# Graph network layers on one core: one-hots of 128-edge tiles built and summed over 64 columns instead of 128

## The chip, the cores and the metric

The kernel runs on one core of a Trainium2 chip. The metric is the time of one execution on the device, in microseconds (us). Five engines work side by side: PE (TensorE, with PEld for its weight loads), DVE (VectorE), ACT (ScalarE), POOL (GpSimd) and SP (SyncE), each with its own instruction stream; semaphores hold them together.

## The reference, cut to what matters

A graph of 6250 nodes with 128 features and 100,000 edges that are sorted by destination goes through two graph-convolution layers, a normalisation, an attention layer over the same edges, and a second normalisation. Each layer sums, for each node, the rows of its edges:

```python
deg = segment_sum(ew, dst)                       # degree, then dinv = rsqrt(deg + 1)
norm = dinv[src] * ew * dinv[dst]                # layers 1 and 2 (with self-loops)
out = segment_sum((x @ W)[src] * norm[:, None], dst) + b
...
e = zs @ aw[0] + zd @ aw[1] + rh @ aw[2]         # attention layer; zs = z[src], rh = r_h @ fc_r_w.T
alpha = softmax of leaky_relu(e) over the edges of a node
agg = segment_sum(alpha[:, None] * (zs + rh), dst)
```

## The kernel before

**Tiles and windows.** The edges are cut into 782 tiles of 128 (T), in 98 groups of 8 (GT, G). Since the edges are sorted, the destinations of one tile lie close together. Each tile t has a window of W = 128 nodes that begins at `base(t)`, 8t - 60, cut at both ends of the graph. `rankC[:, t]` holds for each of the tile's edges its destination less the window's start. A one-hot of a tile is a matrix of 128 edges by 128 window columns, with the edge's weight where the column is its rank. The sum over a tile is one matmul: the 128 gathered rows (or edge features) are the stationary operand, the one-hot is the moving one, and the result is added to 128 columns of a PSUM bank, from `column(t)`.

**Stages.** The *degree pass* builds bf16 one-hots (`SH`, 16 buffers of a group), three groups of four on DVE (L1571) and one on ACT (L1191 and L1195), and sums edge weights with them on PE (L811), in pieces where a window straddles a 512-column bank. ACT copies each closed bank out, and `dinv` and the scaled rows x1 follow. The *first and second pass* (p = 0, 1) are the convolution layers: DVE builds f32 one-hots with weights (`build_S`, L1608, 4 buffers of a group), PE sums with them (`sum_group`, L858). The *third pass* (p = 2) is the attention layer: each tile has two sums, over the gathered rows (L858) and over the edge features (L860), with attention weights that DVE, PE and ACT make per chunk of four groups in front of them.

**Gathers.** The source rows are fetched by POOL with one indirect DMA a tile (L720) into a ring of 18 groups (12 in the third pass); POOL waits until PE has summed the group whose place it needs. The first 18 groups of the first pass are fetched from x itself, ahead of x1; the table of each later pass must be stored first.

**Far sets.** To have fewer gathers, some groups (24 in the first pass, 36 in the second, 12 in the third) are not gathered: their rows are looked up by matmuls with one-hots of source nodes (L898, in the third pass L1033, L1020, L1029) and summed with 288-column one-hots (L1681 on DVE, L910 on PE; in the third pass L1375 and L1380 on ACT, L1045 on PE). These one-hots and sums are not part of the change.

**The general path.** `find_odd` tests on the device whether every rank fits its window (and two other conditions). If not, a flag is set, and a second, general path computes everything anew.

**Order.** The order is written out by hand: each engine's stream loops over groups, with the far sets' steps put between them at fixed groups. The lines to follow are these:

```python
def base(t):
    return min(max(GT * t - MARGIN, 0), NP - W)
...
for j, t in enumerate(tiles(SEQ[gg][1])):                      # build_S, DVE
    last = v.tensor_scalar(S[:, gg % NS, j, :], iota[:, :], rankC[:, t:t + 1], w[:, t:t + 1], ALU.is_equal, ALU.mult)
last.then_inc(s("S_built"), 1)
```

Of the kernel before, what the change touches and what calls it, by code (L numbers as in the profile page):

```python
# [7 lines left out]
ALU = mybir.AluOpType  # L8
ACT = mybir.ActivationFunctionType
AX = mybir.AxisListType  # L10

N, E, D = 6250, 100000, 128
P = 128
W = 128
GT = 8
T = -(-E // P)
G = -(-T // GT)
TC = G * GT
# [7 lines left out]
BW = 512  # L26
NK = -(-NP // BW)
MARGIN = (W - GT) // 2
R = 18
R0 = 18  # L30
NS = 4
NR = 8
ND = 16
# [14 lines left out]
def base(t):  # L48
    return min(max(GT * t - MARGIN, 0), NP - W)

# [2 lines left out]
    return range(q * GT, min((q + 1) * GT, T))  # L53


def pieces(t):

    b, out = base(t), []
    for k in range(b // BW, (b + W - 1) // BW + 1):
        lo, hi = max(b, k * BW), min(b + W, (k + 1) * BW)  # L60
        out.append((k, lo - k * BW, hi - k * BW, lo - b))
    return out

# [12 lines left out]
NA = -(-NP // BA)  # L76
# [16 lines left out]
def column(t):  # L93

    return base(t) - bank_of(t) * BA


OPENS = [min(t for t in range(T) if bank_of(t) == k) for k in range(NA)]
# [139 lines left out]
def build(nc, x, src, dst, edge_attr, edge_weight, W1, b1, W2, b2, fc_w, fc_r_w, attn_w, loop_w, out):  # L238
    ctx = ExitStack()
    with ctx:  # L240
# [19 lines left out]
        iota = sb("iota", [P, P])  # L260
# [4 lines left out]
        iota_h = sb("iota_h", [P, P], BF16)  # L265
        pidx = sb("pidx", [P, 1])
        ident = sb("ident", [P, P])
        ones = sb("ones", [P, P])
# [9 lines left out]

        ring = sb("ring", [P, R, GT, XW])
        rows = sb("rows", [P, NB, XW])  # L280
        SR = sb("SR", [P, NS + NR, GT, W])
        S, rh = SR[:, 0:NS], SR[:, NS:NS + NR]
        SH = SR[:, 0:ND // 2].rearrange("p s t w -> p (s t w)").bitcast(BF16).rearrange("p (s t w) -> p s t w", s=ND, t=GT)
# [13 lines left out]
        rankC = sb("rankC", [P, TC])  # L297
# [71 lines left out]

        setup = ring[:, R - 7:R].rearrange("p s t d -> p (s t d)")  # L370
        lanes = [setup[:, k * EB * P:(k + 1) * EB * P].rearrange("p (b t) -> p b t", t=P) for k in range(5)]
# [4 lines left out]
        tmpC = setup[:, 5 * EB * P + 2 * TC:5 * EB * P + 3 * TC]  # L376
# [38 lines left out]
        ps = [ctx.enter_context(nc.psum_tensor(f"ps{k}", [P, BW], FP32)) for k in range(8)]  # L415
# [3 lines left out]
        def s(name):  # L419
            if name not in sems:  # L420
                sems[name] = sem(name)
            return sems[name]
# [15 lines left out]
        def ring_at(p, h):  # L438

            return (AT[p] + h) % R if p < 2 else GATHERED.index(h) % R2  # L440

# [253 lines left out]
        def _(pool):  # L695
# [5 lines left out]
            nc.gpsimd.memset(rows[:, NB - 1, 0:D], 0.0).then_inc(s("pads_set"), 1)  # L701
            nc.gpsimd.iota(baseI, [[GT, TC]], base=-MARGIN, channel_multiplier=0).then_inc(s("iota_made"), 1)

# [51 lines left out]
        def _(pe):  # L755
# [44 lines left out]
            for q in range(G):  # L800
# [4 lines left out]
                for j, t in enumerate(tiles(q)):  # L805
                    for k, lo, hi, w0 in pieces(t):
                        if t == FIRST[k]:
                            if k >= 2:
                                pe.wait_ge(s("deg_evac"), k - 1)
                            clear(ps[6 + k % 2][0:3, :], 3)  # L810
                        last = nc.tensor.matmul(ps[6 + k % 2][0:3, lo:hi], ewP[:, t, :], SH[:, q % ND, j, w0:w0 + hi - lo],  # L811
                                                start=False, stop=t == LAST[k])
# [29 lines left out]
            def sum_group(p, h):  # L842
                gg = AT[p] + h
                q = SEQ[gg][1]
                parts = PARTS[q] if p < 2 and q in PARTS else (0, len(tiles(q)))
                if p == 2:
                    pe.wait_ge(rh_loaded[q % NR], rh_turns(q))
                pe.wait_ge(s("S_built"), gg + 1)
                near = p < 2 or q in GATHERED
                for j, t in enumerate(tiles(q)):  # L850
                    if near and j in parts:
                        await_rows(pe, p, tiles(q)[j:parts[parts.index(j) + 1]])
                    k = bank_of(t)
                    if t == OPENS[k] and (p == 2 or k + 1 < NA):
                        open_bank(p, k)
                    at, stop = slice(column(t), column(t) + W), t + 1 in OPENS or t + 1 == T and p < 2
                    if near:
                        last = nc.tensor.matmul(ps[(p * NA + k) % 2][:, at], ring[:, ring_at(p, h), j, 0:D], S[:, gg % NS, j, :], start=False, stop=stop)  # L858
                    if p == 2:
                        last = nc.tensor.matmul(ps[2 + k % 2][:, at], rh[:, q % NR, j, :], S[:, gg % NS, j, :], start=False, stop=stop)  # L860
                last.then_inc(s("summed"), 1)

            def count_before(s_, g):
# [312 lines left out]
        def _(act):  # L1176
# [7 lines left out]
            for i, q in enumerate(DEG_ACT):  # L1184
                for k in range(NK):
                    if q - 4 < CLOSE[k] + 3 <= q:
                        evacuate_deg(k)
                if q >= ND:
                    act.wait_ge(s("deg_summed"), q - ND + 1)
                for j, t in enumerate(tiles(q)):  # L1190
                    last = nc.scalar.activation(SH[:, q % ND, j, :], iota_h[:, :], ACT.Abs, bias=rankC[:, t:t + 1], scale=-1.0)  # L1191
                last.then_inc(s("deg_onehot_act"), 1)
                act.wait_ge(s("deg_onehot_act"), 2 * i + 1)
                n = len(tiles(q))
                nc.scalar.activation(SH[:, q % ND, 0:n, :], SH[:, q % ND, 0:n, :], ACT.Relu, bias=ones[:, 0:1], scale=-1.0).then_inc(s("deg_onehot_act"), 1)  # L1195
            for k in range(NK):
                if CLOSE[k] + 3 > DEG_ACT[-1]:
                    evacuate_deg(k)
# [5 lines left out]
            for c in range(0, NB, 7):  # L1204
                for b in range(c + 4, c + 7):
                    last = nc.scalar.activation(rows[:, b, 0:D], rows[:, b, 0:D], ACT.Copy, scale=dinv[:, b:b + 1])
# [257 lines left out]
        def _(dve):  # L1464
            v = nc.vector
            steps = [0]

            def link(ins):

                steps[0] += 1  # L1470
                ins.then_inc(s("dve_step"), 1)
                dve.wait_ge(s("dve_step"), steps[0])
# [20 lines left out]
            at, got = cols_from(0, 1)  # L1493
# [5 lines left out]
            for first, n in ((0, 4), (4, EB - 4)):  # L1499
                at, got = cols_from(first, n)  # L1500
                v.tensor_tensor(rankC[:, at], got, baseT[:, at], ALU.subtract).then_inc(s("cols_copied"), 1)
            for first, n in ((0, 4), (4, EB - 4)):
                at, got = cols_from(first, n)
# [7 lines left out]
            for first, n in ((1, 4), (5, EB - 5)):  # L1511
                at, got = cols_from(first, n)
# [31 lines left out]
            def find_odd():  # L1544

                link(v.tensor_tensor(tmpC, rankC[:, :], baseT, ALU.add))
                link(v.tensor_tensor(dstF.rearrange("p b t -> p (b t)")[:, 0:T - 1], tmpC[:, 0:T - 1], tmpC[:, 1:T], ALU.is_equal))
                link(v.tensor_reduce(odd[:, 0:1], dstF.rearrange("p b t -> p (b t)")[:, 0:T - 1], AX.X, ALU.max))
                link(v.tensor_scalar(tmpC, rankC[:, :], 0.0, None, ALU.is_lt))
                link(v.tensor_reduce(odd[:, 1:2], tmpC[:, 0:T], AX.X, ALU.max))  # L1550
                link(v.tensor_scalar(tmpC, rankC[:, :], float(W), None, ALU.is_ge))
                link(v.scalar_tensor_tensor(tmpC, rankC[:, :], FAR / 2, tmpC, ALU.is_lt, ALU.mult))
                link(v.tensor_reduce(odd[:, 2:3], tmpC[:, 0:T], AX.X, ALU.max))
                link(v.tensor_scalar(dlowI, srcR, P - 1, None, ALU.bitwise_and))
                link(v.tensor_copy(slowH, dlowI))
                link(v.tensor_scalar(dlowI, dstR, P - 1, None, ALU.bitwise_and))
                v.tensor_copy(dlowH, dlowI).then_inc(s("dlo_made"), 1)
                v.tensor_reduce(odd[:, 3:4], odd[:, 0:3], AX.X, ALU.max).then_inc(s("odd_found"), 1)
                dve.wait_ge(s("odd_found"), 1)
                dve.sem_inc(s("setup_done"), 1)  # L1560
# [6 lines left out]
            for q in DEG_DVE:  # L1567
                if q >= ND:
                    dve.wait_ge(s("deg_summed"), q - ND + 1)
                for j, t in enumerate(tiles(q)):  # L1570
                    last = v.tensor_scalar(SH[:, q % ND, j, :], iota_h[:, :], rankC[:, t:t + 1], None, ALU.is_equal)  # L1571
                last.then_inc(s("deg_onehot"), 1)
                if q == 0:
                    weights()
                if q == 2 * ND:
                    find_odd()
# [11 lines left out]
            for i, t0 in enumerate(SAT):  # L1588
                last = v.tensor_scalar(firstC[:, i:i + 1], firstC[:, i:i + 1], float(base(t0)), 0.0, ALU.subtract, ALU.max)
# [3 lines left out]
            for c in range(0, NB, 7):  # L1593
                for b in range(c, c + 4):
                    last = v.tensor_scalar(rows[:, b, 0:D], rows[:, b, 0:D], dinv[:, b:b + 1], None, ALU.mult)
# [7 lines left out]
            def build_S(p, h, w):  # L1603
                gg = AT[p] + h
                if gg >= NS:
                    dve.wait_ge(s("summed"), gg - NS + 1)
                for j, t in enumerate(tiles(SEQ[gg][1])):
                    last = v.tensor_scalar(S[:, gg % NS, j, :], iota[:, :], rankC[:, t:t + 1], w[:, t:t + 1], ALU.is_equal, ALU.mult)  # L1608
                last.then_inc(s("S_built"), 1)

            def make_hi(s_, g):
# [273 lines left out]
            for r, i in enumerate(XR):  # L1885
                last = v.tensor_scalar(dstN[:, r, :], slotD[:, i, :], -1.0, None, ALU.mult)
# [228 lines left out]
            with any_wide(dve):  # L2115
# [16 lines left out]
                for b in range(NB):  # L2132
                    last = v.tensor_scalar(rows[:, b, 0:D], rows[:, b, 0:D], dinv[:, b:b + 1], None, ALU.mult)
# [11 lines left out]
                z = S[:, 1]  # L2145
# [114 lines left out]
```

## Time and profile before

| | |
|---|---|
| median of 3 runs | 2409.7 us (2406.36 to 2409.96) |
| span of the profiled execution, from its first to its last instruction | 3348.6 us |
| mean granted TensorE clock in it | 0.787 |
| PE / DVE / ACT / POOL busy | 2044.2 / 1834.8 / 946.7 / 1718.9 us |
| degree pass, first, second, third pass (begin, us) | about 45, 310, 1180, 2280 |

The profile is of one execution that was recorded instruction by instruction; its span is much longer than the time of a run, and the page gives no other time for it, so its span is its own time here. Busy times are of the profiled execution. The granted clock is the share of 2.4 GHz that TensorE was given: 0.50 is 1.2 GHz, 1.00 is 2.4 GHz.

### The profile page before, as it was taken

To read this page: it belongs to the slowest core of one execution; us is meant where nothing else is said; L and a number is where in the kernel's file an instruction comes from. 1 tells how busy PE (TensorE), PEld (TensorE's weight loads), DVE (VectorE), ACT (ScalarE), POOL (GpSimd) and SP (SyncE) were. 2 spreads that over 40 slices of the span, in tenths; PEclk is the share of its full clock that TensorE was granted. 3 is DMA by queue.
4 is the path that set the end of the run, shared out by engine and by line. 5 is a ranking of instruction groups with operands and counts; after the bars stand their busy time and mean duration, and the time that the engine had idled before them with its cause. 6 is when DMAs were issued, how large, how long until landed. Compare 5 with 4: busy or idle time off the path is not lost.

```text
span 3348.6 us, 40819 instructions
## 1 busy us (share of the span) xinstructions
PE 2044.2 (61%) x13384; PEld 1762.3 (53%) x13384; DVE 1834.8 (55%) x7005; ACT 946.7 (28%) x1754; POOL 1718.9 (51%) x1781
## 2 busy tenths in 40 slices
PE   1416444588888911177777888106677667756786
PEld 1315433566767811166666677005666666645675
DVE  3626435577779810156656687217654564546457
ACT  1316000122233300033333444101254225412541
POOL 7351666665550067466556500555766646663640
PEclk9857667798999955588988899557778778877888
DMA  4112221222221122123333332525343534443431
GB/s 118 30 42 66 69 61 47 61 61 63 60 62 32 51 76 53 41 74 86 99 103 102 93 91 80 138 62 147 97 103 97 134 93 102 108 117 79 103 97 34
DMA packets 272093, 270.54 MB, mean 81 GB/s; under 512 B 43454, under 2 KB 218709, under 8 KB 271862
## 3 DMA queue, kind: packets, MB, share of 16 engines
q1 hardware_dynamic: 201790, 143.87, 15.1%
q0 software_dynamic: 56640, 117.52, 14.8%
q10 hardware_dynamic: 13448, 6.47, 0.7%
q8 instruction: 112, 1.84, 0.2%
q14 instruction: 103, 0.84, 0.1%
HBM read 254.14 MB, written 13.97 MB: 80 GB/s over the span
## 4 chain that ended last, share of the span: by engine, by line
PE 35%; DVE 21%; another core or an unknown queue 21%; issue 15%; ACT 4%; SPq 1%; DMA 1%; POOL 1%; ACTq 0%; DVEq 0%; POOLq 0%
PE ps L858 9%; PE ps L910 8%; DVE SR L1608 5%; PE ps L860 3%; PE ps L898 3%; PE ps L1045 2%; DVE U L1709 2%; DVE SR L1681 2%; DVE SR L1571 1%; PE ps L885 1%; DVE U L1648 1%; PE ps L1029 1%; POOL ring L720 1%; PE ps L792 1%
## 5 line engine op out<-in xcount | busy, mean ns | idle before, releaser
L720 POOL DMA_INDIRECT ring<-x_d,srcC x1132 | 1109.7, 980 | 971.2 <-issue 579.0
L858 PE MATMUL ps<-SR,ring 128*128 128x128 f32 x3540 | 672.5, 320 | 205.0 <-issue 132.0
L858 PEld LDWEIGHTS ps<-SR,ring 128*128 128x128 f32 x3540 | 580.5, 231 | 238.9 <-issue 178.9
L720 POOL DMA_INDIRECT ring<-h_d,srcC x494 | 469.9, 951 | 457.1 <-DMA h_d<-Lb 170.9
L1681 DVE TENSOR_SCALAR SR<-iota_r,cols 128x288 f32<-128x288 f32 x735 | 365.0, 564 | 303.9 <-remote 226.6
L910 PE MATMUL ps<-SR 128*128 128x288 f32 x1470 | 416.6, 435 | 118.1 <-ACT SR L1232 75.3
L910 PEld LDWEIGHTS ps<-SR 128*128 128x128 f32 x1470 | 292.3, 205 | 212.7 <-ACT SR L1232 77.5
L860 PE MATMUL ps<-SR 128*128 128x128 f32 x1564 | 340.3, 312 | 40.8 <-issue 34.6
L1232 ACT COPY SR<-ps 128x512 f32<-128x512 f32 (+1 forms) x195 | 106.0, 561 | 758.4 <-remote 502.9
L860 PEld LDWEIGHTS ps<-SR 128*128 128x128 f32 x1564 | 279.6, 228 | 48.3 <-issue 48.0
L898 PE MATMUL ps<-rows,SR 128*128 128x128 f32 x1470 | 196.2, 285 | 122.5 <-ACT SR L1241 90.6
L898 PEld LDWEIGHTS ps<-rows,SR 128*128 128x128 f32 x1470 | 186.7, 200 | 134.0 <-ACT SR L1241 96.0
L1608 DVE TENSOR_SCALAR SR<-iota,rankC,ewC 128x128 f32<-128x128 f32 x940 | 253.3, 357 | 2.6 <-DVE U L1812 1.1
L1608 DVE TENSOR_SCALAR SR<-iota,rankC,cols 128x128 f32<-128x128 f32 x782 | 213.0, 355 | 14.7 <-issue 11.7
L720 POOL DMA_INDIRECT ring<-in_x_dram,srcC x144 | 137.3, 953 | 93.7 <-issue 90.5
L1571 DVE TENSOR_SCALAR SR<-iota_h,rankC 128x128 bf16<-128x128 bf16 x584 | 107.6, 260 | 125.9 <-issue 106.1
L1709 DVE SCALAR_TENSOR_TENSOR U<-SR,v2B 128x128 f32<-128x128 f32 x686 | 156.0, 286 | 34.3 <-DVE U L1709 18.1
L1239 ACT ACTIVATE SR<-SR,negp 128x512 bf16<-128x512 bf16 (+1 forms) x195 | 134.9, 692 | 112.0 <-remote 100.3
L811 PE MATMUL ps<-SR,cols 128*3 128x128 bf16 (+2 forms) x974 | 74.0, 237 | 110.7 <-issue 57.0
L1241 ACT ACTIVATE SR<-SR,negp 128x512 f32<-128x512 bf16 (+1 forms) x195 | 135.9, 697 | 6.4
L1963 DVE TENSOR_TENSOR_SCAN U<-U,ps 32x384 f32<-32x384 f32 (+2 forms) x27 | 25.4, 942 | 203.8 <-remote 115.7
L811 PEld LDWEIGHTS ps<-SR,cols 128*3 128x3 bf16 x974 | 60.0, 96 | 123.5 <-issue 65.0
(288 smaller groups left out, 2703.4 us busy)
## 6 DMA issues: line engine op xcount, KB each, us to landing
SR<-in_edge_attr_dram SPq DMA_DIRECT2D x97, 512.0 KB
SR<-low_d SPq DMA_DIRECT2D x90, 256.0 KB
U<-dlo_d SPq DMA_DIRECT2D x74, 256.0 KB
ring<-x_d,srcC POOLq DMA_INDIRECT x1132
ring<-h_d,srcC POOLq DMA_INDIRECT x494
SR<-dlo_d SPq DMA_DIRECT2D x12, 512.0 KB
ring<-in_edge_attr_dram SPq DMA_DIRECT2D x12, 512.0 KB
U<-lo_d SPq DMA_DIRECT2D x18, 256.0 KB
```

Of the source, the lines that this page charges most:

```text
L720: pool.indirect_dma_start(ring[:, ring_at(p, h if p < 2 else q), k, 0:width], None, (x if p == 0 and h < R0 else table)[:, :], bass.Indire ...
L811: last = nc.tensor.matmul(ps[6 + k % 2][0:3, lo:hi], ewP[:, t, :], SH[:, q % ND, j, w0:w0 + hi - lo], start=False, stop=t == LAST[k])
L858: last = nc.tensor.matmul(ps[(p * NA + k) % 2][:, at], ring[:, ring_at(p, h), j, 0:D], S[:, gg % NS, j, :], start=False, stop=stop)
L860: last = nc.tensor.matmul(ps[2 + k % 2][:, at], rh[:, q % NR, j, :], S[:, gg % NS, j, :], start=False, stop=stop)
L898: last = nc.tensor.matmul(ps[3 + m % 2][:, i * P:(i + 1) * P], ohS[:, m % 2, i * P:(i + 1) * P], rows[:, a, 0:D], start=True, stop=True)
L910: nc.tensor.matmul(ps[5][:, SLACK:SPAN], rowX[:, m % 2, i * P:(i + 1) * P], slotS[:, n % NQ, :], start=False, stop=a == NB - 1).then_inc(s ...
L1239: nc.scalar.activation(low, low, ACT.Abs, bias=negp[:, 0:1]).then_inc(s("low_apart"), 1)
L1241: return nc.scalar.activation(out, low, ACT.Relu, bias=negp[:, 1:2], scale=-1.0)
L1571: last = v.tensor_scalar(SH[:, q % ND, j, :], iota_h[:, :], rankC[:, t:t + 1], None, ALU.is_equal)
L1608: last = v.tensor_scalar(S[:, gg % NS, j, :], iota[:, :], rankC[:, t:t + 1], w[:, t:t + 1], ALU.is_equal, ALU.mult)
L1681: v.tensor_scalar(slotS[:, n % NQ, :], iota_up, slotD[:, RUNS[i], a:a + 1], slotW[:, RUNS[i], a:a + 1], ALU.is_equal, ALU.mult).then_inc(s ...
L1709: v.scalar_tensor_tensor(junk[:, n % NJ, :], attr, 1.0, v2B[:, :], ALU.mult, ALU.mult, accum_out=s2C[:, t:t + 1]).then_inc(s("rh_dotted"), 1)
```

## The change

Inner tiles (all but the first and last eight) get a narrower view of their window, its columns 32 to 95. One-hots are built over these 64 columns alone and summed into these 64 alone; edge tiles keep 128. This holds in the degree pass (DVE, ACT and PE, whose pieces are cut from the view) and in the three passes (`build_S` and `sum_group`). The windows' starts, the banks and their order, the number of one-hots and of sums in the three passes and the far sets stay. `find_odd` compares the ranks of inner tiles with 32 and 96 in place of 0 and 128, with three instructions for each of the two tests in place of one, so that the general path is taken where the narrow view would miss an edge.

```diff
+NEAR, EDGE = W // 4, GT
...
+def view(t):
+
+    return (NEAR, W - NEAR) if EDGE <= t < T - EDGE else (0, W)
...
     b, out = base(t), []
-    for k in range(b // BW, (b + W - 1) // BW + 1):
-        lo, hi = max(b, k * BW), min(b + W, (k + 1) * BW)
+    a, z = (b + w for w in view(t))
+    for k in range(a // BW, (z - 1) // BW + 1):
+        lo, hi = max(a, k * BW), min(z, (k + 1) * BW)
...
-                    at, stop = slice(column(t), column(t) + W), t + 1 in OPENS or t + 1 == T and p < 2
+                    lo, hi = view(t)
+                    at, stop = slice(column(t) + lo, column(t) + hi), t + 1 in OPENS or t + 1 == T and p < 2
                     if near:
-                        last = nc.tensor.matmul(ps[(p * NA + k) % 2][:, at], ring[:, ring_at(p, h), j, 0:D], S[:, gg % NS, j, :], start=False, stop=stop)
+                        last = nc.tensor.matmul(ps[(p * NA + k) % 2][:, at], ring[:, ring_at(p, h), j, 0:D], S[:, gg % NS, j, lo:hi], start=False, stop=stop)
                     if p == 2:
-                        last = nc.tensor.matmul(ps[2 + k % 2][:, at], rh[:, q % NR, j, :], S[:, gg % NS, j, :], start=False, stop=stop)
+                        last = nc.tensor.matmul(ps[2 + k % 2][:, at], rh[:, q % NR, j, :], S[:, gg % NS, j, lo:hi], start=False, stop=stop)
...
-                    last = nc.scalar.activation(SH[:, q % ND, j, :], iota_h[:, :], ACT.Abs, bias=rankC[:, t:t + 1], scale=-1.0)
+                    lo, hi = view(t)
+                    last = nc.scalar.activation(SH[:, q % ND, j, lo:hi], iota_h[:, lo:hi], ACT.Abs, bias=rankC[:, t:t + 1], scale=-1.0)
...
-                nc.scalar.activation(SH[:, q % ND, 0:n, :], SH[:, q % ND, 0:n, :], ACT.Relu, bias=ones[:, 0:1], scale=-1.0).then_inc(s("deg_onehot_act"), 1)
+                nc.scalar.activation(SH[:, q % ND, 0:n, lo:hi], SH[:, q % ND, 0:n, lo:hi], ACT.Relu, bias=ones[:, 0:1], scale=-1.0).then_inc(s("deg_onehot_act"), 1)
...
-                link(v.tensor_scalar(tmpC, rankC[:, :], 0.0, None, ALU.is_lt))
+                for a, z in ((0, EDGE), (EDGE, T - EDGE), (T - EDGE, TC)):
+                    last = v.tensor_scalar(tmpC[:, a:z], rankC[:, a:z], float(view(a)[0]), None, ALU.is_lt)
+                link(last)
...
-                    last = v.tensor_scalar(SH[:, q % ND, j, :], iota_h[:, :], rankC[:, t:t + 1], None, ALU.is_equal)
+                    lo, hi = view(t)
+                    last = v.tensor_scalar(SH[:, q % ND, j, lo:hi], iota_h[:, lo:hi], rankC[:, t:t + 1], None, ALU.is_equal)
...
-                    last = v.tensor_scalar(S[:, gg % NS, j, :], iota[:, :], rankC[:, t:t + 1], w[:, t:t + 1], ALU.is_equal, ALU.mult)
+                    lo, hi = view(t)
+                    last = v.tensor_scalar(S[:, gg % NS, j, lo:hi], iota[:, lo:hi], rankC[:, t:t + 1], w[:, t:t + 1], ALU.is_equal, ALU.mult)
```

## Rows read from the trace of the kernel before

**Rows 1.** The page, part 1: busy us, share of span, instructions.

```profile
PE 2044.2 (61%) x13384; PEld 1762.3 (53%) x13384; DVE 1834.8 (55%) x7005; ACT 946.7 (28%) x1754; POOL 1718.9 (51%) x1781
```

**Rows 2.** The page, part 4: chain that ended last, by engine, by line.

```profile
PE 35%; DVE 21%; another core or an unknown queue 21%; issue 15%; ACT 4%; SPq 1%; DMA 1%; POOL 1%; ACTq 0%; DVEq 0%; POOLq 0%
PE ps L858 9%; PE ps L910 8%; DVE SR L1608 5%; PE ps L860 3%; PE ps L898 3%; PE ps L1045 2%; DVE U L1709 2%; DVE SR L1681 2%; DVE SR L1571 1%; PE ps L885 1%; DVE U L1648 1%; PE ps L1029 1%; POOL ring L720 1%; PE ps L792 1%
```

**Rows 3.** Timeline of DVE, then PE: start us, us, operation, count, idle before.

```profile
107.34 22.52 DVE L1571 TENSOR_SCALAR SR<-iota_h,rankC 128x128 bf16<-128x128 bf16 x138 [0.45 <-issue]
...
188.40 0.26 DVE L1571 TENSOR_SCALAR SR<-iota_h,rankC 128x128 bf16<-128x128 bf16 x1 [1.01 <-issue]
189.80 0.26 DVE L1571 TENSOR_SCALAR SR<-iota_h,rankC 128x128 bf16<-128x128 bf16 x1 [1.15 <-issue]
...
1215.76 0.37 PE L898 MATMUL ps<-rows,SR 128*128 128x128 f32 x1 [2.43 <-issue]
```

**Rows 4.** Timeline of POOL, the start of the second pass: one gather.

```profile
1194.79 0.94 POOL L720 DMA_INDIRECT ring<-h_d,srcC  x1 [0.30 <-issue]
```

**Rows 5.** Groups by line: busy us, mean ns, idle us before and releasers.

```profile
L720 POOL DMA_INDIRECT ring<-x_d,srcC x1132 | 1109.7, 980 | 971.2 <-issue 579.0 <-PE ps L860 175.2 <-remote 129.4
L858 PE MATMUL ps<-SR,ring 128*128 128x128 f32 x3540 | 672.5, 320 | 205.0 <-issue 132.0 <-DVE SR L1608 54.7 <-remote 11.0
L860 PE MATMUL ps<-SR 128*128 128x128 f32 x1564 | 340.3, 312 | 40.8 <-issue 34.6 <-DVE SR L1608 6.0
L1608 DVE TENSOR_SCALAR SR<-iota,rankC,ewC 128x128 f32<-128x128 f32 x940 | 253.3, 357 | 2.6 <-DVE U L1812 1.1 <-issue 0.3
...
L1571 DVE TENSOR_SCALAR SR<-iota_h,rankC 128x128 bf16<-128x128 bf16 x584 | 107.6, 260 | 125.9 <-issue 106.1 <-remote 19.4
```

**Rows 6.** Windows: us; PE, PEld, DVE, ACT, POOL busy (x); granted clock, DMA, GB/s.

```profile
700.00:1180.00 480.00, 401.62 (x2544) 344.92 (x2544) 365.82 (x1119) 149.37 (x270) 180.49 (x186) 0.93 0.20 55
1400.00:2095.00 695.00, 548.19 (x3481) 464.29 (x3482) 456.31 (x1503) 272.19 (x429) 311.30 (x326) 0.89 0.33 90
2310.00:3300.00 990.00, 685.66 (x4134) 610.27 (x4134) 560.46 (x2575) 368.60 (x703) 561.36 (x569) 0.79 0.40 103
```

**Rows 7.** Groups by line and shape, DVE: other widths.

```profile
L1681 DVE TENSOR_SCALAR SR<-iota_r,cols 128x288 f32<-128x288 f32 x735 | 365.0, 564 | 303.9 <-remote 226.6 <-PE ps L910 77.1
L1825 DVE TENSOR_SCALAR U<-U,pidx 128x1024 bf16<-128x1024 bf16 x74 | 33.1, 483 | 97.4 <-remote 87.2 <-PE ps L944 6.3 <-DMA U<-dlo_d 3.5
...
L1802 DVE SCALAR_TENSOR_TENSOR s1C<-U,ds,s1n 128x16 f32<-128x16 f32 x48 | 8.5, 231 | 0.9 <-DVE ds L1797 0.3
```

**Rows 8.** Timeline of PE in the degree pass: one group's sums.

```profile
141.28 1.01 PE L811 MATMUL ps<-SR,cols 128*3 128x128 bf16 x8 [6.57 <-DVE SR L1571]
```

**Rows 9.** Timeline of PE, third pass: a stretch of narrow and wide matmuls.

```profile
2727.16 3.65 PE L1029 MATMUL ps<-ring 128*128 128x49 f32 x16
2730.61 3.75 PE L860 MATMUL ps<-SR 128*128 128x128 f32 x16
2734.15 2.12 PE L1029 MATMUL ps<-ring 128*128 128x49 f32 x16
2736.10 2.02 PE L860 MATMUL ps<-SR 128*128 128x128 f32 x16
2738.25 1.09 PE L1029 MATMUL ps<-ring 128*128 128x49 f32 x8
2740.17 1.09 PE L1029 MATMUL ps<-ring 128*128 128x49 f32 x8 [0.83 <-ACT ring L1363]
2741.10 3.42 PE L860 MATMUL ps<-SR 128*128 128x128 f32 x16
```

**Rows 10.** Chain by line in 700:1180, 1400:2095 and 2310:3300 us, in this order.

```profile
by line: PE ps L910 17.9%; PE ps L858 13.7%; another core or an unknown queue 8.5%; PE ps L885 6.9%; PE ps L898 6.6%; DVE SR L1608 6.5%; issue 5.5%; DVE SR L1681 4.3%; DVE U L1648 4.2%; PE ps L872 3.6%; DVE U L1637 2.2%; PE ps L840 2.0%; PE
by line: PE ps L910 26.1%; PE ps L858 15.9%; issue 11.9%; another core or an unknown queue 10.3%; PE ps L898 9.5%; DVE SR L1608 4.5%; DVE SR L1681 3.5%; ACT SR L1239 2.1%; PE ps L944 1.4%; PE ps L840 1.3%; SPq L505 1.0%; ACT L1293 0.9%; ACT
by line: issue 17.8%; another core or an unknown queue 13.5%; PE ps L858 9.5%; PE ps L860 9.4%; PE ps L1045 6.6%; DVE U L1709 5.5%; DVE SR L1608 5.0%; PE ps L1029 2.7%; PE ps L1033 2.5%; PE ps L1020 2.2%; DVE U L1970 1.6%; DVE U L1972 1.6%;
```

More of the change, by code:

```diff
@@ L1548, in find_odd @@
                 link(v.tensor_reduce(odd[:, 0:1], dstF.rearrange("p b t -> p (b t)")[:, 0:T - 1], AX.X, ALU.max))
-                link(v.tensor_scalar(tmpC, rankC[:, :], 0.0, None, ALU.is_lt))
+                for a, z in ((0, EDGE), (EDGE, T - EDGE), (T - EDGE, TC)):
+                    last = v.tensor_scalar(tmpC[:, a:z], rankC[:, a:z], float(view(a)[0]), None, ALU.is_lt)
+                link(last)
                 link(v.tensor_reduce(odd[:, 1:2], tmpC[:, 0:T], AX.X, ALU.max))
-                link(v.tensor_scalar(tmpC, rankC[:, :], float(W), None, ALU.is_ge))
+                for a, z in ((0, EDGE), (EDGE, T - EDGE), (T - EDGE, TC)):
+                    last = v.tensor_scalar(tmpC[:, a:z], rankC[:, a:z], float(view(a)[1]), None, ALU.is_ge)
+                link(last)
                 link(v.scalar_tensor_tensor(tmpC, rankC[:, :], FAR / 2, tmpC, ALU.is_lt, ALU.mult))
```

## The prediction

> **What bounds the kernel now.** I read the page's busy line first, then its chain of waits, then the gathers one by one, then each stage with its clock. No engine is full: PE is busy 61% of the span, DVE 55%, POOL 51% [rows 1]. The span, 3348.6 us, is not the time of a run: the three runs have a median of 2409.7 us (2406.36 to 2409.96), 939 us less. The chain shows where such an excess can lie: 21% of it is "another core or an unknown queue" and 15% "issue" [rows 2], together 1229 us that belong to no engine's work. While POOL gathers without a break, DVE steps once in 1.40 us with "issue" before each step, and PE pauses 2.43 us before one matmul; where POOL is held up, DVE issues 138 one-hots in 22.52 us, 163 ns each [rows 3]. I read these pauses as the price of recording and not as work. So engine work on the chain carries over into a run in full, and "issue" and "unknown" do not: terms are worked out in the profiled span and added to 2409.7 us unscaled.
>
> A gather is issued every 1.25 us (0.94 us and a gap of 0.30) [rows 4], also when nothing holds it up. There are 1770 of them (1132 from x1 and x2 [rows 5], and two more rows of L720 with 494 and 144): 1770 x 1.25 = 2212 us. If that holds in a run, only 198 us of the 2409.7 us are left for all times in which POOL waits. The gathers are thus a floor that no engine's saving gets under, and a cover that can swallow small changes of PE or DVE. Above that floor PE and DVE take turns: in 700 to 1180 us (the second half of the first pass) PE is busy 402 of 480 us and DVE 366; in the third pass 686 and 560 of 990 [rows 6].
>
> **What the change removes, on DVE.** build_S (L1608) has 1866 instructions: 940 of them in one row [rows 5], 782 and 144 in two more. Sixteen edge tiles in each of three passes keep 128 columns, so 1818 shrink. A 128-column one costs 253.3 us / 940 = 269 ns of busy time. No row shows 64 columns of this kind. From the 16-column two-operation row (8.5 us / 48 = 177 ns) the slope is 0.82 ns a column, a saving of 53 ns; from the 288-column row (365.0 / 735 = 497 ns) it is 1.42 ns, a saving of 91 ns [rows 7]. I take 60, nearer the row with the same plain columns, since the 288-column one reads a reversed view. DVE's busy time falls by 1818 x 60 ns = 109 us (bounds 96 and 165). Only what is on the chain counts: L1608 is 5% of it [rows 2], 164 us, of which 60/269 go: **-37 us** (bounds: 0 if the gathers cover it, -109 if every build is in the way).
>
> In the degree pass L1571 takes 107.6 us / 584 = 184 ns for 128 bf16 columns [rows 5], and 33.1 us / 74 = 447 ns for 1024 [rows 7]: 0.29 ns a column, 19 ns for 64, 11 us in all. It is 1% of the chain, 44 us, of which 19/184 go: **-5 us** (bounds 0 and -11; zero if the 144 gathers ahead, 180 us, end after this stage does). PE's degree matmuls get narrower and fewer (974 pieces become 880, counted from the tiles' bounds, since fewer windows straddle a bank), and ACT's one-hots shrink too. Both are costed at nothing: PE is waiting for DVE's one-hots there (6.57 us before one group) [rows 8], and ACT has a quarter of the groups. If that cover were gone they would give some us more. find_odd gains four small instructions, under 0.3 us each by the 16-column row's 231 ns [rows 7]: **+1 us**.
>
> **What it does not remove, on PE.** The sums (L858 and L860, 3540 + 1564 instructions [rows 5]) keep their stationary operand, 128 columns of f32 rows; only the moving one-hot shrinks. The row to read is a stretch where sixteen matmuls with 49 moving columns alternate with sixteen of 128: 3.65 and 3.75 us at the one clock, 2.12 and 2.02 us at the other [rows 9]. A matmul with 49 columns takes as long as one with 128. So 64 columns take as long as 128, and PE's sums save **0 us**.
>
> A page gives another figure. The Trainium skill, "TensorE: Matmul & The Clock Gate", section "Back-to-back issue gap", has the gap of matmuls follow the moving columns, 134 cycles for 128 and about 60 for 64; by it the sums would lose about half of their PE time. The trace does not agree: 2.12 against 2.02 us.
>
> **What it may cost, on PE's clock.** The same rows show something worse. At 1.2 GHz sixteen 49-column matmuls ran back to back for 3.65 us, and the clock was still 1.2 GHz after them (the next sixteen took 3.75 us); after those sixteen of 128 columns it was 2.4 GHz. Then two batches of eight 49-column matmuls ran with a gap of 0.83 us, and the 128-column ones behind them took 3.42 us, the low clock again [rows 9]. Narrow matmuls keep PE as occupied as wide ones but do not hold the clock up. The granted clock is 0.93 in 700 to 1180 us, 0.89 in the second pass, 0.79 in the third [rows 6]. The first two also have sums of 288 columns (L910) and look-ups of 128 (L898), which stay; the third is mostly L858 and L860. I take 0.91, 0.86 and 0.69: in the third pass a third of the way down to 1.2 GHz (0.50), because its far sets (L1045, L1033) still bring wide matmuls in 39 of 98 groups (three rounds of 13 look-ups in the code). PE's lines on the chain [rows 10] are, in the order of stages, 51% of 480 us (L910, L858, L885, L898, L872, L840) = 243 us; 54% of 695 (L910, L858, L898, L944, L840) = 377; 33% of 990 (L858, L860, L1045, L1029, L1033, L1020) = 326. Cost: 243 x (0.93/0.91 - 1) = 5; 377 x (0.89/0.86 - 1) = 13; 326 x (0.79/0.69 - 1) = 47: **+65 us**. Bounds: 0 if the clock stays, 326 x (0.79/0.50 - 1) = 189 us in the third pass if it runs at 1.2 GHz throughout.
>
> The Trainium skill, same page, section "Part 1: The HAM clock gate", says the clock follows how busy the PE has recently been. By that rule sixteen narrow matmuls back to back would raise the clock as sixteen wide ones do, this term would be zero and the time that of the first rival, 2369 us. The rows speak against it, though no row here has 64 columns.
>
> **Sum:** -37 - 5 + 1 + 65 = +24 us: 3348.6 becomes 3373 in a profiled run, and 2409.7 becomes 2434 us in a timed one. I forecast 2434.
>
> **The rivals.**
> *The clock holds and DVE's saving shows* (faster). 64 columns are more than 49, and in a run without the recording pauses the matmuls stand closer, which holds the clock. Then the sum is -41: 2369 us. For it: PE waits on L1608 54.7 us at L858 [rows 5]. Against it: the rows of 49 columns. It decides if the third pass's clock stays above about 0.74: there 326 x (0.79/0.74 - 1) = 22 us and the 18 us of the other stages together eat DVE's 41. If all of DVE's 109 + 11 us counted, the time would be 2290 us, but POOL's 2212 us and its waits at the ends of three passes (an estimate: some 30 us each) leave little under 2300.
> *The gathers cover both.* If POOL is the floor in the second and third pass, a shorter DVE and a slower PE both vanish behind it, since the ring holds 18 groups (12 in the third pass). For it: 2212 of 2409.7 us. Against it: in the trace POOL waits for L860 175.2 us [rows 5]. Time: 2405 to 2414 us.
> *PE's sums get cheaper after all.* At 2.4 GHz sixteen sums take 2.02 us [rows 9], 126 ns each; if 64 columns halved that, 5000 instructions would give 315 us, and the gathers' floor would stop it at about 2300 us. Against it: the 49-column rows. (The Trainium skill's figure for the gap, above, would have it so.)
> *The general path is taken.* Not with these inputs: worked out from the reference's setup, the ranks in inner tiles lie between 55 and 86, inside 32 to 95. Under 1 in 100, and then many times the time.
>
> **How the numbers follow.** Forecast (the clock falls by more than DVE saves): 0.48, its own range 2415 to 2520. Clock holds: 0.34, 2300 to 2404. Covered: 0.15. Cheaper sums: 0.03. Faster is 0.34 + 0.03 = 0.37, same 0.15, slower 0.48; a change within 0.2% (4.8 us) can't be told from none. For 8 in 10 I leave out about a tenth on each side: below 2340 us (most of DVE's saving and cheaper sums) and above 2505 us (about half of the bound of 189 us for the third pass).
>
> **What would show it.** L1608 at about 210 ns busy each instead of 269, L1571 at 165; sixteen L858 in about 2.0 us at the high clock and 3.6 at the low one as now; the granted clock of the third pass near 0.69, of the first two within 0.03 of now; more POOL waits for L858 and L860. The prediction is wrong if the clock of the third pass stays at 0.79, if sixteen sums take visibly less than 2 us at the high clock, or if POOL's gathers fill the run so that nothing moves.

## The result, and the profile after

The changed kernel takes a median of 2475.78 us in five runs (2470.48 to 2479.55), the kernel before 2408.41 us beside it (2405.29 to 2409.96). The ratio is 1.0274 with a 95% interval of 1.0258 to 1.029: 66 us slower. The forecast was 24 us slower, so the sign and the range hold and the size does not.

The profile of the changed kernel has a span of 2474.0 us, which is the time of its run. First the page: its busy line, its line of granted clocks in 40 slices, its chain by engine, and groups by line.

```profile
PE 2049.2 (83%) x13290; PEld 1823.9 (74%) x13290; DVE 1751.1 (71%) x7009; ACT 928.4 (38%) x1754; POOL 1745.8 (71%) x1781
...
PEclk9975789799999689889999965556866589556876
...
PE 46%; DVE 21%; POOL 16%; issue 9%; ACT 3%; DMA 3%; SPq 1%; ACTq 0%; DVEq 0%; POOLq 0%
...
L866 PE MATMUL ps<-SR,ring 128*128 128x64 f32 (+1 forms) x3540 | 671.9, 327 | 65.9 <-DVE SR L1623 35.3
...
L868 PE MATMUL ps<-SR 128*128 128x64 f32 (+1 forms) x1564 | 379.8, 346 | 5.7 <-DVE SR L1623 5.7
...
L1623 DVE TENSOR_SCALAR SR<-iota,rankC,ewC 128x64 f32<-128x64 f32 (+1 forms) x940 | 224.4, 336 | 2.2 <-DVE U L1827 0.6
```

The rows of before that stand ahead of the prediction cannot be set beside these, because that execution was stretched to 3348.6 us [rows 1 to 3]. I took that for the price of recording. It was not: a second profile of the same kernel has a span of 2402.3 us, and every comparison below is with it. The same lines of its page:

```profile
PE 1834.3 (76%) x13384; PEld 1623.4 (68%) x13384; DVE 1815.0 (76%) x7005; ACT 946.3 (39%) x1754; POOL 1749.5 (73%) x1781
...
PEclk9878899999999899999999995778897889779988
...
POOL 40%; PE 21%; issue 17%; DVE 12%; DMA 8%; ACT 1%; SPq 1%; ACTq 0%; POOLq 0%; DVEq 0%
...
L858 PE MATMUL ps<-SR,ring 128*128 128x128 f32 x3540 | 613.8, 305 | 105.0 <-DVE SR L1608 55.5
...
L860 PE MATMUL ps<-SR 128*128 128x128 f32 x1564 | 320.1, 300 | 6.0 <-DVE SR L1608 6.0
L1608 DVE TENSOR_SCALAR SR<-iota,rankC,ewC 128x128 f32<-128x128 f32 x940 | 254.9, 360 | 2.2 <-DVE U L1812 0.5
```

Three things are to be seen. In an undisturbed execution the chain of before is POOL's: 40%, and most of the 17% "issue" is the 0.30 us between two gathers. After the change PE holds 46% of it. The narrow sums are busy for longer than the wide ones (671.9 + 379.8 against 613.8 + 320.1 us), and the clock line falls to 5 and 6 in the third pass. DVE's one-hots fall from 254.9 / 940 = 271 ns to 239.

Now the passes by windows, from the first sum to the last (columns as in [rows 6]). Before, measured again:

```profile
155.00:809.00 654.00, 545.37 (x3905) 482.07 (x3904) 553.66 (x1711) 172.81 (x312) 477.86 (x475) 0.91 0.28 79
828.00:1448.00 620.00, 528.35 (x3595) 459.39 (x3594) 462.85 (x1517) 276.42 (x434) 466.76 (x484) 0.93 0.43 120
1503.00:2391.00 888.00, 645.62 (x4467) 589.29 (x4468) 604.08 (x2820) 381.18 (x727) 650.95 (x658) 0.85 0.48 126
```

After:

```profile
147.00:808.00 661.00, 581.79 (x3906) 516.26 (x3905) 534.88 (x1711) 172.77 (x312) 478.07 (x480) 0.85 0.30 79
827.00:1446.00 619.00, 546.22 (x3595) 471.52 (x3594) 448.60 (x1512) 276.21 (x435) 464.08 (x484) 0.90 0.43 119
1506.00:2462.00 956.00, 810.75 (x4468) 747.10 (x4468) 580.13 (x2814) 383.85 (x727) 654.98 (x658) 0.67 0.46 116
...
1515.00:1680.00 165.00, 134.97 (x614) 128.69 (x615) 94.64 (x437) 41.15 (x85) 126.90 (x126) 0.50 0.44 111
...
1877.00:1977.00 100.00, 88.89 (x394) 82.53 (x394) 65.64 (x302) 34.26 (x74) 77.14 (x76) 0.50 0.45 109
```

The loss is the third pass: 956 against 888 us, at a clock of 0.67 against 0.85. It has stretches of 100 us and more that run wholly at 1.2 GHz (0.50), with PE busy 82 to 89% of the time.

POOL's timeline shows where such a slower PE becomes time. Columns are start, length, operation, and the idle time before it. Before, measured again, the last gather of a pass and the first of the next:

```profile
776.40 0.98 POOL L720 DMA_INDIRECT ring<-x_d,srcC  x1 [0.30 <-issue]
814.92 0.95 POOL L720 DMA_INDIRECT ring<-h_d,srcC  x1 [37.54 <-issue]
...
1441.44 0.95 POOL L720 DMA_INDIRECT ring<-h_d,srcC  x1 [0.30 <-DMA ring<-h_d,srcC]
1465.03 1.10 POOL L720 DMA_INDIRECT ring<-x_d,srcC  x1 [22.63 <-issue]
...
2354.22 0.96 POOL L720 DMA_INDIRECT ring<-x_d,srcC  x1 [0.30 <-issue]
```

After:

```profile
769.27 1.83 POOL L727 DMA_INDIRECT ring<-x_d,srcC  x1 [0.30 <-issue]
813.95 0.94 POOL L727 DMA_INDIRECT ring<-h_d,srcC  x1 [42.86 <-issue]
...
1437.35 0.94 POOL L727 DMA_INDIRECT ring<-h_d,srcC  x1 [0.30 <-issue]
1466.74 1.10 POOL L727 DMA_INDIRECT ring<-x_d,srcC  x1 [28.45 <-issue]
...
2366.66 0.94 POOL L727 DMA_INDIRECT ring<-x_d,srcC  x1 [0.30 <-issue]
```

Inside a pass the gathers run at one per 1.25 us in both kernels. At the end of a pass POOL has nothing to do until PE has worked off the groups that lie in the ring and the pass's rows are stored. I call this time the drain. For the third pass it is the time from the start of the last gather (2354.22 and 2366.66) to the end of PE's last sums (2391.7 and 2462.9), which are these, before and after:

```profile
2391.36 0.39 PE L860 MATMUL ps<-SR 128*128 128x128 f32 x2
...
2462.22 0.64 PE L868 MATMUL ps<-SR 128*128 128x128 f32 x2
```

How far PE is behind can be counted: from the last gather on, it has some 165 of the third pass's sums still to start before the change, and some 370 after. The drains of all kernels profiled (of one execution each), in us, and each kernel's ratio to before (of its timed runs):

| kernel | first | second | third | sum | ratio (95%) |
|---|---|---|---|---|---|
| before, again | 38.5 | 23.6 | 37.5 | 99.6 | 1 |
| the change | 44.7 | 29.4 | 96.2 | 170.3 | 1.0274 (1.0258 to 1.029) |
| builds 64, sums 128 | 33.7 | 22.6 | 34.3 | 90.6 | 0.993 (0.9908 to 0.9952) |
| the same, second time | 28.0 | 22.9 | 35.7 | 86.6 | 0.9936 (0.9923 to 0.995) |
| builds 128, sums 64 | 78.9 | 32.1 | 93.6 | 204.6 | 1.0386 (1.0341 to 1.0432) |
| third pass 128 | 62.6 | 28.4 | 45.3 | 136.3 | 1.0059 (1.0035 to 1.0082) |
| degree pass alone 64 | 41.0 | 22.4 | 42.3 | 105.7 | 1.0001 (0.9988 to 1.0013) |
| 96 in place of 64 | 46.1 | 30.7 | 42.3 | 119.1 | 0.9997 (0.9981 to 1.0014) |
| change + one-row matmuls | 63.8 | 27.6 | 150.4 | 241.8 | 1.1292 (1.1246 to 1.1338) |
| change + 128-row matmuls | 63.8 | 28.4 | 71.6 | 163.8 | 1.0206 (1.0186 to 1.0226) |
| builds 40, sums 128 | 33.7 | 21.6 | 35.3 | 90.6 | 0.9926 (0.9908 to 0.9943) |
| builds 64 in first pass alone | 32.6 | 23.4 | 38.5 | 94.5 | 0.9955 (0.9943 to 0.9967) |
| builds 64 in third pass alone | 41.5 | 24.6 | 33.1 | 99.2 | 1.0001 (0.9993 to 1.001) |

The change adds 170.3 - 99.6 = 71 us of drain, and the two profiled spans differ by 2474.0 - 2402.3 = 72 us. The stretches between the drains nearly cancel: the gathers of the first pass end 7 us earlier, those of the second take 3 us less and those of the third 11 us more. Drains of one kernel differ by some 5 us between profiles (33.7 and 28.0 above), so smaller differences in the table are not read.

### The profile page after: what moved, and what is told of

Its sections match the earlier page's. It is cut to its first block, busy times and chain, and to the rows that moved or that the text cites. A ratio compares the mean times of both kernels' runs of the same rounds, so it can differ in the third digit from the quotient of the medians.

```text
span 2474.0 us, 40635 instructions
## 1 busy us (share of the span) xinstructions
PE 2049.2 (83%) x13290; PEld 1823.9 (74%) x13290; DVE 1751.1 (71%) x7009; ACT 928.4 (38%) x1754; POOL 1745.8 (71%) x1781
## 4 chain that ended last, share of the span: by engine, by line
PE 46%; DVE 21%; POOL 16%; issue 9%; ACT 3%; DMA 3%; SPq 1%; ACTq 0%; DVEq 0%; POOLq 0%
POOL ring L727 16%; PE ps L866 13%; PE ps L918 9%; PE ps L868 6%; DVE SR L1623 4%; DVE SR L1585 4%; PE ps L906 3%; PE ps L893 2%; DVE SR L1696 2%; PE ps L1053 2%; PE ps L1037 2%; DVE U L1663 1%; PE ps L799 1%; DMA ring<-x_d,srcC 1%; PE ps L847 1%
## 5 line engine op out<-in xcount | busy, mean ns | idle before, releaser
L727 POOL DMA_INDIRECT ring<-x_d,srcC x1132 | 1126.3, 995 | 381.2 <-issue 364.3
L866 PE MATMUL ps<-SR,ring 128*128 128x64 f32 (+1 forms) x3540 | 671.9, 327 | 65.9 <-DVE SR L1623 35.3
L866 PEld LDWEIGHTS ps<-SR,ring 128*128 128x128 f32 x3540 | 607.2, 243 | 89.5 <-issue 48.2
L868 PE MATMUL ps<-SR 128*128 128x64 f32 (+1 forms) x1564 | 379.8, 346 | 5.7 <-DVE SR L1623 5.7
L918 PEld LDWEIGHTS ps<-SR 128*128 128x128 f32 x1470 | 294.3, 206 | 82.8 <-issue 3.6
L868 PEld LDWEIGHTS ps<-SR 128*128 128x128 f32 x1564 | 320.7, 260 | 6.0 <-issue 5.8
L1623 DVE TENSOR_SCALAR SR<-iota,rankC,ewC 128x64 f32<-128x64 f32 (+1 forms) x940 | 224.4, 336 | 2.2 <-DVE U L1827 0.6
L1623 DVE TENSOR_SCALAR SR<-iota,rankC,cols 128x64 f32<-128x64 f32 (+1 forms) x782 | 185.7, 331 | 7.1 <-PE ps L868 5.8
L1053 PE MATMUL ps<-ring 128*128 128x288 f32 x294 | 104.8, 512 | 0.0
L799 PE MATMUL ps<-iota_r,zero_h 1*128 1x512 bf16 (+1 forms) x128 | 58.8, 484 | 51.2 <-DVE SR L1623 34.1
L1663 DVE TENSOR_SCALAR U<-iota,U 128x128 f32<-128x128 f32 x288 | 61.0, 298 | 54.7 <-PE ps L893 54.7
```

The costliest lines, as they stand in the source:

```text
L727: pool.indirect_dma_start(ring[:, ring_at(p, h if p < 2 else q), k, 0:width], None, (x if p == 0 and h < R0 else table)[:, :], bass.Indire ...
L918: nc.tensor.matmul(ps[5][:, SLACK:SPAN], rowX[:, m % 2, i * P:(i + 1) * P], slotS[:, n % NQ, :], start=False, stop=a == NB - 1).then_inc(s ...
L1053: nc.tensor.matmul(ps[5][:, SLACK:SPAN], rowX2[:, m % 2, j * P:(j + 1) * P], slotX[:, n % NQ2, :], start=False, stop=a == NB - 1).then_inc ...
L1623: last = v.tensor_scalar(S[:, gg % NS, j, lo:hi], iota[:, lo:hi], rankC[:, t:t + 1], w[:, t:t + 1], ALU.is_equal, ALU.mult)
```

## The experiments

**The kernel before once more.** No edit.

> The kernel before once more, unchanged, for a profile of its own. My reading in the prediction (the long span of 3348.6 us is the price of recording): the pauses come again and the span is again some 3300 us. Rival (that one execution was stretched by something else): the span comes out at about 2406 us, like the 2474.0 us of the changed kernel beside its 2475.8 us, and the stages can then be set side by side.

Its span is 2402.3 us, its time 2404.21. The rival holds: the pauses of [rows 3] belonged to that one execution. The shares of its chain [rows 2, 10], which sized three of my terms, describe no ordinary run.

**Builds narrow, sums wide.**

```
 sum_group:
-                    lo, hi = view(t)
+                    lo, hi = 0, W
 build_S:
+                wide = gg < NS or any(view(t) == (0, W) for t in tiles(SEQ[gg - NS][1]))
-                    lo, hi = view(t)
+                    lo, hi = (0, W) if wide else view(t)
```

> One-hots are still built in 64 columns by DVE (in 128 in the first four groups and after an edge group, so that the outer columns hold zeros), but PE sums over all 128. Theory 1 (narrow sums lower the clock, and that is the loss): the clock of the third pass comes back to what the kernel before has, DVE keeps its saving of about 30 ns an instruction (269 to 239 ns), and the time is at or under the one before: 2375 to 2410 us. Theory 2 (the narrow builds or their strided one-hots cost, whatever PE does): it stays at 2450 us or above.

The degree pass stays narrow. 2389.93 us against 2406.07: as theory 1 has it, and faster than both kernels. In its third pass PE's clock is 0.84 and its busy time 652 us, near the 646 of before:

```profile
1495.00:2385.00 890.00, 652.08 (x4470) 596.69 (x4471) 581.69 (x2818) 381.34 (x727) 656.70 (x658) 0.84 0.47 125
```

Theory 2 falls.

**Builds wide, sums narrow.**

```
 build_S:
-                    lo, hi = view(t)
+                    lo, hi = 0, W
```

> DVE builds all 128 columns again, PE sums over the middle 64 alone. Theory 1 (clock): the clock of the third pass stays at the 0.67 of the changed kernel, DVE's saving is lost on top, and the time is 2475 to 2530 us. Theory 2 (narrow builds cost): the loss is gone, 2400 to 2420 us.

2505.45 us, the third pass at 0.69. Narrow sums (beside the narrow degree pass, which is worth nothing by a run below) cost 3.9%; the narrow builds of the change give some of it back.

**Third pass wide.**

```
 sum_group:
-                    lo, hi = view(t)
+                    lo, hi = view(t) if p < 2 else (0, W)
 build_S:
-                    lo, hi = view(t)
+                    lo, hi = view(t) if SEQ[gg][0] < 2 else (0, W)
```

> The third pass goes back to 128 columns in builds and sums; degree pass and the first two passes keep 64. Theory 1 as the prediction had it (nearly all of the clock's cost lies in the third pass, which has few other wide matmuls): the third pass's clock rises from 0.67 to near 0.8 and the time is 2385 to 2425 us. Rival (the loss is spread over all three passes, since the clock falls in the first two as well): a third to a half of the loss comes back, 2440 to 2460 us.

2422.62 us: the third pass's clock is back at 0.84, and most of the loss is gone (2.74% becomes 0.59%). What stays lies mostly in the first drain, 62.6 us at a clock of 0.83 in the first pass. With the same code up to there, the changed kernel's profile had 44.7 us and two later kernels 63.8, so that this drain is not the same from run to run; why is not known.

**The degree pass alone.** The two edits of the last two runs together: both lines set to `0, W` for all passes.

> Only the degree pass is narrow; builds and sums of all three passes keep 128 columns. Theory now (POOL's gathers, one per 1.25 us, set the pace; work on other engines shows only in the drains, the time from the last gather of a pass to the first of the next): the drains are as before (39, 24 and 37 us), the degree pass is 9 us shorter but PE has caught up with the gathers long before the first pass ends, so the time is within 5 us of before: 2400 to 2406 us. Rival (the degree pass's 8 to 9 us show in full, and are the whole gain of the run with narrow builds and wide sums): 2390 to 2398 us.

2407.56 against 2407.99 us: nothing, as the gathers' pace has it. The first sum starts 8 us earlier (147 in place of 155 us), and the first pass's last gather is issued at 774 us in place of 776.

**More work for PE in the third pass, one row deep.** Ahead of the sums of 81 groups, 648 more instructions on PE in all:

```
 sum_group:
+                k = bank_of(q * GT)
+                if p == 2 and q * GT != OPENS[k]:
+                    for _ in range(8):
+                        nc.tensor.matmul(ps[2 + k % 2][:, :], zero_h[0:1, 0:P],
+                                         iota_r[0:1, 0:BW // 2].bitcast(BF16), start=False, stop=False)
```

> The changed kernel with more work for PE: ahead of each group of the third pass (but those that open a bank) eight matmuls of 512 bf16 columns that add zeros to a bank in use; nothing else differs. Theory 1 (the narrow sums cost only because TensorE's clock is low under them): the third pass's clock rises from 0.67 to 0.8 or more, the last drain falls from 95 us to 40 to 55 us, and the kernel gets faster by working more: 2405 to 2435 us. Rival (the sums over 64 columns are slow by themselves, or PE is simply full): the clock may rise, but the time does not fall, 2475 us or, with 90 groups of 8 x 0.21 us more work for PE, up to 2620 us.

2712.25 us, above even the rival's 2620. The clock did not rise: 0.62 over the pass. In PE's timeline the eight run at 1.2 GHz, and so do the sums behind them (two matmuls in 0.64 us):

```profile
1605.72 3.59 PE L858 MATMUL ps<-iota_r,zero_h 1*128 1x512 bf16 x8
...
1609.72 0.64 PE L872 MATMUL ps<-SR 128*128 128x64 f32 x2
```

So this run did not test theory 1: the cause that it was meant to change, the clock, stayed where it was. It showed that in such a pass most of PE's work is paid for: 648 x 3.59 / 8 us = 291 us of it made the kernel 236 us slower than the changed one.

**The same work, 128 rows deep.** Operands `zero_h[:, :]` and `iota_r[:, 0:BW // 2]`, all else as in the last run.

> As the run with more work, but the eight zero matmuls ahead of each group use all 128 rows of the array in place of one (128x128 zeros against 128x512 bf16): the same columns, the same duration. The run with one row showed eight of them back to back in 3.59 us at 1.2 GHz without a rise of the clock, at 2712 us. Theory 1, sharpened (what holds the clock up is work of many columns on many rows): the clock of the third pass rises to 0.8 or more, the drain after the last gather falls from 95 to 40 to 60 us, and the time from the 2712 us to 2405 to 2450 us, less than the changed kernel without this work. Rival (the clock follows something else, or PE is full whatever its clock): 2600 to 2720 us again.

2457.32 us: 255 us less than with one row, and 0.7% under the changed kernel by the ratios to before (1.0206 against 1.0274), though PE does 648 matmuls more. The third pass as a window, then its timeline:

```profile
1523.00:2445.00 922.00, 773.21 (x5051) 639.32 (x5121) 581.02 (x2816) 382.30 (x727) 650.79 (x658) 0.87 0.48 121
```

```profile
1567.84 1.67 PE L858 MATMUL ps<-iota_r,zero_h 128*128 128x512 bf16 x7
1569.35 0.33 PE L870 MATMUL ps<-SR,ring 128*128 128x64 f32 x2
1569.52 0.39 PE L872 MATMUL ps<-SR 128*128 128x64 f32 x2
```

At the granted clock of 0.87 two sums of 64 columns take 0.39 us in place of 0.64. The time missed my 2405 to 2450 us. The drains say why: 71.6 us in the third pass in place of 40 to 60, because the added matmuls are themselves 648 x 0.216 = 140 us of PE's time (0.216 is 1.51 us / 7 in the timeline; the eighth has no record there), and 63.8 us in the first pass, which keeps its narrow sums. Against the changed kernel's profile the first drain is 19 us longer, though the code up to there is the same; the third pass alone is 35 us shorter (24.6 us of drain and 10.5 of gathers).

**96 columns.** `NEAR = W // 8`.

> 96 columns (16 to 112) in place of 64 in the degree pass and all passes. If a matmul's columns hold the clock up step by step (theory 1), the third pass's clock lies between 0.67 and 0.85, the last drain between 37 and 95 us, and the time between the two kernels: 2405 to 2445 us. Rival (any narrowing below 128 costs the clock in full, or the cost is in straddling or strided one-hots): 2460 to 2480 us.

2406.66 us, no change; the third pass's clock is 0.82 and its drain 42 us. I read it as what the narrow builds give and what the clock takes cancelling; no run takes the two apart at 96 columns.

**Builds narrow, sums wide, again.** The kernel of the second run.

> Narrow builds and wide sums once more, beside the run with the degree pass alone: the pair tells what narrow builds are worth in the passes. By the gathers' pace: drains 5 and 4 us shorter than before at the ends of the first and third pass, 2388 to 2397 us, and 4 to 12 us less than with the degree pass alone. Rival (builds are hidden altogether): the same time as the degree pass alone, within 3 us.

2390.91 us, 0.64% (0.5 to 0.77) under before. Beside the degree pass alone this puts the narrow builds in the passes at some 15 us, more than the 4 to 12 that I expected.

**Builds over 40 columns.** `view` returns `(48, 88)` for inner tiles (in the degree pass too), sums wide.

> Builds over 40 columns (48 to 88, the narrower bound flagged as before), sums over 128. If DVE's time shows in the drains of the first and third pass (narrow builds of 64 gave 17 us there for 33 ns saved in an instruction), another 12 ns give some 6 us: 2382 to 2388 us. Rival (the drains have reached what PE and the stores take): the same as with 64 columns, 2389 to 2394 us.

2389.98 us: a miss, and as the rival has it. One-hots get shorter again (213.7 / 940 = 227 ns in place of 239), and the time does not move.

**Builds narrow in one pass alone**, first or third; degree pass and sums wide.

```
 build_S (the first alone; != 2 for the third):
+                    lo, hi = (0, W) if wide or SEQ[gg][0] != 0 else view(t)
```

> Narrow builds (64 columns) in the first pass alone; degree pass, all sums and the builds of the other two passes keep 128. The profiles put the gain of 17 us of narrow builds at the end of the first pass (the drain there is 28 to 34 us in place of 39 to 41) and at the end of the third. If that is so: 8 to 12 us under before, 2395 to 2400 us. Rival (the gain is spread over the passes, or needs the short degree pass as well): 2401 to 2407 us.

> Narrow builds in the third pass alone, all else 128 columns. By the profiles' last drains (33 to 35 us after the last gather in place of 37 to 42): 3 to 8 us under before, 2399 to 2404 us. Rival (builds of the third pass are hidden behind the gathers): no change, 2405 to 2409 us.

The first pass alone gives 2395.39 us, 0.45% (0.33 to 0.57), as expected. The third alone gives nothing (2408.04 us, 1.0001), where I expected 3 to 8 us from its profile's shorter last drain. So two thirds of the gain of narrow builds is made in the first pass. Where the remaining 4 us come from, the second pass or the sum of small parts, stays open.

## Why the prediction was right in sign and wrong in size

**The term that failed: DVE's -37 us, with -5 for the degree pass.** The sum -37 - 5 + 1 + 65 = +24 became about -15 + 81 = +66, the 81 being what the measured 66 leaves beside the 15. Both DVE terms came from shares of the chain of an execution that was not an ordinary run [rows 2]. In an undisturbed profile L1608 is 3% of the chain and POOL's gathers lead it. All narrow builds and the degree pass together give 15 us (0.9936) in place of 42: some 11 in the first pass and none in the third. The degree pass gives 0, which my lower bound named (the gathers cover it). Each saving was also mis-sized: 271 - 239 = 32 ns an instruction and not 60. I had taken 60 / 64 = 0.94 ns a column, between the slopes of two neighbours, 0.82 and 1.42 [rows 7]; the measured one, 32 / 64 = 0.50, lies below both.

**The clock term was right in kind and too small: +65 became some +81 us** (1.0274 / 0.9936 = 1.034 of 2391 us; 3.9% or 93 us with wide builds). The step that was too small is the fall of the third pass's clock. I took it a third of the way down to 0.50, from 0.79 to 0.69; it went half of the way, from 0.85 to 0.67. That 0.67 lies near my 0.69 is luck, since 0.79 belonged to the stretched execution. The first pass, given 0.91, ran at 0.85; I had expected its wide sums to hold it up. But the way in which the clock costs time was not the one I summed, PE's share of the chain. PE falls behind the gathers, unseen while the ring has room, and pays at the end: the third drain grows by 59 us. Before that POOL is held up a little: its gathers of the third pass take 2366.66 - 1466.74 = 900 us in place of 2354.22 - 1465.03 = 889, and 8.1 us of that are waits for L868.

**PE's sums save 0: right.** Sums of 64 columns take 0.39 us a pair at 2.4 GHz and 0.64 at 1.2, which is what pairs of 128 columns take in the kernel before, measured again:

```profile
2381.53 0.64 PE L860 MATMUL ps<-SR 128*128 128x128 f32 x2
...
2391.36 0.39 PE L860 MATMUL ps<-SR 128*128 128x128 f32 x2
```

*Cheaper sums* is refuted. The prediction took only the table by columns from the section of the Trainium skill that it names ("TensorE: Matmul & The Clock Gate", "Back-to-back issue gap"). The section gives that table for matmuls taken singly, and says that in a stream in which each matmul has its own weight load both set the spacing. The trace agrees with that as far as it goes: each of these sums has its own weight load (13290 of each in the page), and its spacing does not follow the columns.

**The clock holds: refuted for 64-column sums, right for 128.** The prediction's mark for it was a clock of 0.74 in the third pass. With wide sums the pass has 0.84 and the kernel is faster, 2390 us, though less than the rival's 2369. The Trainium skill, same page, "Part 1: The HAM clock gate", has the clock follow how busy the PE has been. The trace does not agree: PE was busy 82% of 165 us (134.97) and stayed at 0.50, while in the same stretch before, measured again, it was busy 63% (103.66) at 0.77:

```profile
1515.00:1680.00 165.00, 103.66 (x698) 96.59 (x698) 110.14 (x514) 43.65 (x89) 126.65 (x126) 0.77 0.45 117
```

**The gathers cover both: half right.** They cover what DVE saves in the third pass and the degree pass's 8 us. They do not cover a slower PE, since its arrears come due at the end of each pass. The figure of 1.25 us a gather carried over from the stretched profile and holds in every run while nothing holds POOL up.

**The signs named beforehand.** L1571's successor takes 87.9 / 584 = 151 ns (165 forecast); before, measured again, L1571 took 96.9 / 584 = 166 and not 184. More waits of POOL for the sums: only 8.1 us for L868. They show instead as "issue" at the ends of passes, which I had not thought to read.

## What to carry to other kernels

Before sizing terms by shares of a chain, check that the profile's span is near the time of a run; if it is not, take another profile, since such shares belong to that execution alone. Where one queue paces the work through a deep ring, price a change by how far the others are behind it when a stage ends, not by the busy time that it saves. A one-hot may be built over fewer columns than the matmul reads, as long as the rest holds zeros: here that gave 0.6%, and narrowing the matmul as well turned it into a loss of 2.7%.

## What the runs showed of the hardware

- In the stretch of 165 us that ran wholly at 1.2 GHz, 416 of PE's 614 matmuls were f32 sums of 64 columns and 132 had 49, each with new weights. The clock came up behind wide ones: eight of 288 columns took 4.21 us and eight of 128 then 1.67, and the 64-column pairs after them 0.39 us in place of 0.64.

```profile
1700.36 4.21 PE L1053 MATMUL ps<-ring 128*128 128x288 f32 x8
1704.37 1.67 PE L1041 MATMUL ps<-rows,ring 128*128 128x128 f32 x8
1705.87 0.33 PE L866 MATMUL ps<-SR,ring 128*128 128x64 f32 x2
1706.04 0.39 PE L868 MATMUL ps<-SR 128*128 128x64 f32 x2
```

- Eight bf16 matmuls of 512 columns ahead of a group did not bring the clock up when one row deep (0.62 over the pass) and did when 128 rows deep (0.87), with zeros as weights in both.
- A one-hot of two operations on DVE took 271, 239 and 227 ns busy for 128, 64 and 40 columns: most of it does not shrink.
